# Prologue of a transformer-layer kernel: row normalisation behind its own moments, x loaded first, rotation table in two parts

## What is computed

```python
def _layernorm(x, axis=-1, eps=1e-05):
    return (x - mean(x)) / sqrt(var(x) + eps)
...
q, k, v = proj(Wq, bq), proj(Wk, bk), proj(Wv, bv)
q, k = _apply_rope(q, sin, cos), _apply_rope(k, sin, cos)      # rotation by position
scores = where(pos < 205 or pos >= 1536, q @ k.T * scale, -inf)
attn_out = softmax(scores) @ v @ Wo.T + bo
...
logits = x @ router_w.T
expert, weight = argmax(logits), softmax(top2(logits))[0]
out_e = (silu(x @ gate_w.T) * (x @ up_w.T)) @ down_w.T          # of that expert
...
x = x + attn(xn) + weight * out_e(xn)
```

## Time and profile before

| | us |
|---|---|
| median of 3 runs | 395.14 |
| lowest, highest | 394.01, 395.59 |
| profiled execution | 396.47 |
| its span, first to last instruction | 394.7 |

### The profile page before, as it was taken

How to read it: one execution, slowest core, us unless ns; L and a number is a source line. 1 busy time by engine, 2 the same in 40 slices (tenths; PEclk the granted TensorE clock), 3 DMA queues, 4 the chain that set the end, 5 groups by cost and what they waited for, 6 DMA issues and landing times.

```text
span 394.7 us, 12245 instructions
## 1 busy us (share of the span) xinstructions
PE 370.9 (94%) x4646; PEld 194.1 (49%) x4646; DVE 322.2 (82%) x549; ACT 270.2 (68%) x537; POOL 65.6 (17%) x82
## 2 busy tenths in 40 slices
PE   0999999999999999999999999999999999997896
PEld 0765566766655443444444444445454444432265
DVE  5769789997759888988888888888888898874566
ACT  2534666564448878778787787878888888886910
POOL 5003734431000213032130321300000000000000
PEclk9999999999999999999999999999999999998999
DMA  7998556755111213032130321302102022095626
GB/s 238 407 384 215 145 169 200 215 171 157 41 58 54 70 32 95 11 94 63 41 88 14 99 55 46 92 11 71 55 21 70 25 52 56 17 204 105 101 54 213
DMA packets 30920, 42.53 MB, mean 108 GB/s; under 512 B 10724, under 2 KB 25700, under 8 KB 30048
## 3 DMA queue, kind: packets, MB, share of 16 engines
q1 hardware_dynamic: 29000, 36.71, 32.5%
q0 software_dynamic: 1872, 5.11, 5.1%
HBM read 27.75 MB, written 13.67 MB: 105 GB/s over the span
## 4 chain that ended last, share of the span: by engine, by line
PE 83%; DMA 5%; DVE 4%; issue 3%; ACT 2%; SPq 2%; DVEq 0%; ACTq 0%
PE ps L735 19%; PE ps L713 18%; PE ps L653 17%; PE ps L601 7%; PE ps L528 5%; PE ps L614 5%; PE ps L772 4%; DVE mx L1025 3%; DMA softmax_sums<-o_st 2%; DMA bqk<-bqk_in 2%; PE ps L639 2%; PE ps L517 1%; PE ps L587 1%; PE ps L626 1%; PE ps L510 1%
## 5 line engine op out<-in xcount | busy, mean ns | idle before, releaser
L1025 DVE TENSOR_REDUCE mx<-ps 128x1 f32<-128x717 f32 x232 | 198.6, 899 | 30.6 <-PE ps L653 30.1
L735 PE MATMUL ps<-q_op,k_op 98*32 98x512 bf16 (+1 forms) x1472 | 129.7, 383 | 3.6 <-DMA q_op<-neg_row 1.6
L1307 ACT ACTIVATE probs<-ps 128x512 f32<-128x512 f32 x192 | 103.1, 598 | 19.9 <-PE ps L735 18.1
L653 PE MATMUL ps<-k_op,q_op 96*32 96x512 bf16 (+1 forms) x1856 | 111.2, 315 | 0.4 <-DVE mx L1025 0.3
L653 PEld LDWEIGHTS ps<-k_op,q_op 96*32 96x32 bf16 x1856 | 50.7, 96 | 56.3 <-issue 25.3
L735 PEld LDWEIGHTS ps<-q_op,k_op 98*32 98x32 bf16 (+1 forms) x1472 | 42.3, 96 | 67.0 <-ACT probs L1307 15.0
L713 PE MATMUL ps<-probs,v_op 128*32 128x512 f32 x384 | 50.6, 595 | 0.2 <-ACT o_st L1298 0.2
L1307 ACT ACTIVATE dn<-ps 77x512 f32<-77x512 f32 x64 | 34.8, 595 | 11.6 <-PE ps L735 11.6
L457 POOL COPY v_op<-v_all 128x192 f32<-128x192 f32 x16 | 7.0, 446 | 202.7 <-PE ps L713 202.7
L1307 ACT ACTIVATE gu<-ps 128x512 f32<-128x512 f32 x64 | 34.5, 599 | 9.1 <-PE ps L735 9.1
L1307 ACT ACTIVATE wqk<-ps 128x512 f32<-128x512 f32 x64 | 33.5, 599 | 8.1 <-PE ps L735 8.1
(11 more groups left out here) (127 smaller groups left out, 366.0 us busy)
## 6 DMA issues: line engine op xcount, KB each, us to landing
q_parts<-parts SPq DMA_DIRECT2D x12, 256.0 KB
sorted_results<-ys SPq DMA_DIRECT2D x23, 128.0 KB
q_op<-q_parts SPq DMA_DIRECT2D x15, 192.0 KB
gu<-gu_in SPq DMA_DIRECT2D x1, 2816.0 KB, 13.7
tab<-tab_in SPq DMA_DIRECT2D x1, 2048.0 KB, 11.6
sorted_rows<-xn SPq DMA_DIRECT2D x4, 512.0 KB, 6.1
out<-x_sb SPq DMA_DIRECT2D x8, 256.0 KB, 2.4
q_op<-q_parts SPq DMA_DIRECT2D x15, 128.0 KB
```

The lines of the kernel that those rows point to most:

```text
L653: ins = pe.matmul(ps[r:r + CW, at + c0:at + c0 + n], q_op[slot][0:KR, P * t + r:P * t + r + CW], k_op[slot][0:KR, c0:c0 + n], start=True, ...
L735: ins = pe.matmul(bank(4 + u % RING)[r:r + w, :], k_op[k][:, c0 + r:c0 + r + w], q_op[k][:, QB * b:QB * b + QB], start=True, stop=True)
L1025: dve.tensor_reduce(mx[:, slot, t:t + 1], ps[:, at:at + NK], AX.X, ALU.max).then_inc(max_reduced, 1)
L1307: act.activation(prob[c][0:rows, QB * b:QB * b + QB], bank(4 + u % RING)[0:rows, :], ACT.Exp, scale=SCALE).then_inc(exp_done, 1)
```

## The change

It does six things, all in the prologue and at its edge to the expert stage.

1. DVE's `moments` is split in `moments` (statistics) and `variance`; group 0 is normalised right behind its own variance, and the others one half step later. `ON_DVE = (1, 1, 2, 2)` tiles of the groups are normalised by DVE, the others by ACT (3, 3, 2, 2; before 2, 2, 2, 0), and ACT counts each tile by itself.
2. All of x is issued ahead of the other loads, but for the identity (128 columns of `const`), which goes third. The rest of `const` follows behind the key weights.
3. `wqk` is loaded as keys (ahead) and queries (last of the row); the value weights no longer share a semaphore with the biases.
4. `tab` is loaded as the columns that the keys need (205 and 512, 717 KB together) and, behind the wait for `xs_in[1]` on SP, the 1331 columns between (1331 KB). DVE waits for these ahead of `times_cos(2)`.
5. PE does the logits of rows 0 to 511 behind pair 1, `project(0)` behind pair 2, and one chunk of values behind each of pairs 3 and 4.
6. POOL fills `v_all` with ones first, then the rows of the key operands.

```diff
@@ loads, SP
+                if g == 0:
+                    sp.dma_start(const[:, C_ID:C_ID + P], const_d[:, C_ID:C_ID + P]).then_inc(ident_in, 16)
...
+            tab_v = tab_d.rearrange("p (a n) -> p a n", a=2)
+            for c0, c1 in ((0, START), (S - RECENT, S)):
+                sp.dma_start(tab[:, :, c0:c1], tab_v[:, :, c0:c1]).then_inc(key_tab_in, 16)
...
             sp.wait_ge(xs_in[1], 16)
+            sp.dma_start(tab[:, :, START:S - RECENT], tab_v[:, :, START:S - RECENT]).then_inc(tab_in, 16)
             sp.dma_start(wo[:], wo_d).then_inc(wo_in, 16)
@@ POOL
+            pool.memset(v_all[:], 1.0).then_inc(ones_ready, 1)
+            pool.wait_ge(ones_ready, 1)
             for n in range(RING):
                 pool.memset(k_op[n][KR:KM, :], 1.0).then_inc(ones_ready, 1)
...
-            pool.memset(v_all[:], 1.0).then_inc(ones_ready, 1)
@@ turn_pair, PE
+                g = pair // 2
+                if pair % 2 == 0:
+                    pe.wait_ge(xn_ready, g + 1)
+                pe.wait_ge(xn_on_act, ON_ACT[g] + 2 - ON_DVE[g] if pair % 2 == 0 else ON_ACT[g + 1])
@@ DVE
-            for g in range(1, 4):
-                moments(g)
-                normalize(g - 1)
+            variance(0)
+            normalize(0)
+            moments(1)
+            variance(1)
+            moments(2)
+            normalize(1)
+            variance(2)
+            moments(3)
+            normalize(2)
+            variance(3)
             normalize(3)
...
             turn(1)
+            dve.wait_ge(tab_in, 16)
             times_cos(2)
@@ ACT
             root(0)
-            for g in range(1, 4):
-                root(g)
-                normalize(g - 1)
-                copy_xT(2 * g - 2)
-                copy_xT(2 * g - 1)
+            normalize(0)
+            copy_xT(0)
+            root(1)
+            copy_xT(1)
+            normalize(1)
+            root(2)
+            copy_xT(2)
+            copy_xT(3)
+            normalize(2)
+            root(3)
+            copy_xT(4)
+            normalize(3)
+            copy_xT(5)
             copy_xT(6)
```

More of the change, by code:

```diff
@@ L65 @@
 EARLY_MAX = 6 * 512
+ON_DVE = (1, 1, 2, 2)
+ON_ACT = [sum(4 - n for n in ON_DVE[:g]) for g in range(5)]
 EARLY_TILES = [(0, t) for t in range(NT)] + [(1, t) for t in range(NT // 2)]
@@ L531, in project @@
                     ins.then_inc(proj_ready, 1)
-            pe.wait_ge(const_in, 16)
-            for pair in range(NT // 2):
-                turn_pair(pair)
[L536 to L543, removed]
-                        logits_part(0, m)
-            pe.wait_ge(wv_in, 32)
-            project_v(V_ORDER[0])
+            pe.wait_ge(ident_in, 16)
+            turn_pair(0)
+            turn_pair(1)
+            pe.wait_ge(rt_in, 16)
+            pe.wait_ge(xnT_ready, 2)
+            for m in range(HC):
+                logits_part(0, m)
+            turn_pair(2)
+            pe.wait_ge(wk_in, 32)
+            project(0)
+            turn_pair(3)
+            pe.wait_ge(wv_in, 16)
+            project_v(V_ORDER[0])
+            turn_pair(4)
+            project_v(V_ORDER[1])
+            for pair in range(5, NT // 2):
+                turn_pair(pair)
             for b in range(1, NQB):
@@ L807, in moments, with variance @@
                     step(dve.bn_stats(stats[:, t, :], x_sb[:, t, :]))
+            def variance(g):
                 settle()
@@ L820, in normalize @@
                                          rstd[:, 4 * g:4 * g + 4], ALU.mult, ALU.mult).then_inc(scale_ready, 1)
[L822 removed]
+                for t in range(4 * g, 4 * g + ON_DVE[g]):
                     ins = dve.tensor_scalar(xn[:, t, :], x_sb[:, t, :], mv[:, t, 0:1], rstd[:, t:t + 1],
@@ L1190, in normalize @@
                 act.wait_ge(scale_ready, g + 1)
-                for t in range(4 * g + 2, 4 * g + 4):
-                    ins = act.activation(xn[:, t, :], x_sb[:, t, :], ACT.Identity, bias=shift[:, t:t + 1],
-                                         scale=rstd[:, t:t + 1])
-                ins.then_inc(xn_on_act, 1)
+                for t in range(4 * g + ON_DVE[g], 4 * g + 4):
+                    act.activation(xn[:, t, :], x_sb[:, t, :], ACT.Identity, bias=shift[:, t:t + 1],
+                                   scale=rstd[:, t:t + 1]).then_inc(xn_on_act, 1)
             def biased(u, odd):
```

37 lines of the change are left out of this document (15 added, 22 removed).

## The result

The changed kernel takes 398.33 us (median of 6, 397.68 to 400.27) against 394.69 us (6, 393.13 to 395.59) for the kernel before in the same rounds: a ratio of 1.0102, 95% interval 1.0070 to 1.0134. That is 3.6 us more, where +0.7 was forecast, and beyond the range's end of 397.7. On another chip it was 398.75 to 395.10, a ratio of 1.0096 [1.0067, 1.0125].

A forecast was written before the change was run, and what follows sets the result against it. TensorE was taken as the bound, unbroken from 12.19 us. The larger of -0.35 (prologue) and +0.7 (late table) was added to 395.14, giving 395.8 us; range 393.7 to 397.7.

The forecast's parts named there:

- the table's landing: Edge to expert stage: the table's middle lands at 45.4 us, between 44.8 and 46.8, and VectorE waits for it.
- the issue: SyncE issues the table's middle when the second gather has landed: 39.5 us, between 39.2 and 40.6.
- the duration: Transfer of the table's middle, 1331 KB: 5.9 us, between 5.6 and 6.2.
- rival 3: Table's middle takes 7.5 us amid gathers and key stores, landing at 48.1 if issued at 40.6: 398.5 us; chance 0.14.
- The slack: VectorE's idle time at the expert stage: `times_cos(2)` may start 3.05 us later, at 44.7, with nothing late.
- Whatever is beyond goes through in full: Expert stage: any table delay past 44.7 us reaches TensorE in full, since TensorE gives nothing back from 66 us.
- the larger of two: The end moves by the larger of the prologue's -0.35 us and the table's +0.7 us.
- The head: Prologue: transposes of the logits at 24.05 instead of 24.40 us, 0.35 gained, between -0.9 and +1.1.
- GpSimd's part: Start of prologue: VectorE's variance waits for GpSimd's filling of `v_all`; filled first, variance ends at 5.7 to 5.9, not 6.57.
- 1 (table in time): Expert-stage edge: a 5.1 us transfer or quicker gather leaves the prologue's gain standing, 394.0 to 394.8 us; chance 0.25.
- 2 (the whole early start): Prologue: early clock rise and early `rt` keep TensorE 2.8 us ahead, table in time: 392.3 us; chance 0.08.
- 4: Prologue: ScalarE's order and a late clock lose 0.9 us, gather late, table at 46.6: 397.0 us; chance 0.08.

The follow-up runs named there:

- t1: Changed kernel with the table's middle loaded in two transfers, the 307 columns read first ahead of the other 1024: ratio 1.0013 to the kernel before.
- b0: Kernel before, unchanged, run and profiled a second time: 394.12 us, ratio 0.9983.
- a1: Changed kernel with the table's middle issued at the end of the first row of loads, not behind the second gather: ratio 1.0053 to the kernel before.
- p1: a1 with 24 more, long fulfilled waits on SyncE ahead of the row stores: ratio 1.0017 to the kernel before.
- g1: f1 with router weights behind x's second group, expert down weights behind the second gather, and 24 more fulfilled SyncE waits: ratio 1.0064 to the kernel before.
- u1: f1 with router weights behind x's second group and only 307 middle table columns early, 1024 behind the second gather: 393.59 us, ratio 0.9954.
- f1: a1 with ScalarE normalising ahead of copies, pairs 4 to 7 turned in a row, value chunks placed where TensorE waited: ratio 1.0036 to the kernel before.

## Why the prediction was wrong, point by point

**The step that failed is the table's landing.** Forecast 45.4 with an upper bound of 46.8, measured 48.02, so TensorE lost 2.76 us to it and not 0.7. Two terms: the issue, forecast 39.5, was 40.33, because the second gather was issued at 37.01 instead of 36.3 (head) and took 3.30 instead of some 3.2; and the duration, forecast 5.9 [5.6, 6.2], was 7.69. The duration is the larger miss. I had built it from `wo`'s 3.0 us, for a fifth of the bytes, and the increments of loads in the first row, where no gather runs. The row nearest in kind was the whole table's, 11.6 us amid other traffic, whose share is 7.5; I used it for rival 3 alone and let the range end short of it. That rival (issued 40.6, 7.5 us, landing 48.1, 398.5 us) is what happened. The Trainium skill ("DMA: Bandwidth & Descriptors", Anatomy of one DMA), whose fit is for transfers that GpSimd issues while SyncE issues this one, gave an estimate of 5.1 us, further off still than my 5.9 from the measured 7.69.

**The slack** of 3.05 us was nearly right. Nothing is late up to a `times_cos(2)` at 45.28, which is 3.6 us behind 41.67 and 0.6 more than I took; t1, at 45.60, has a lag no larger than its prologue's. "Whatever is beyond goes through in full" and "the larger of two" held: in four profiles the lag is the start less 45.28, whatever the prologue did. The earlier trace rows carried this part.

**The head** was forecast at -0.35 and came out at +0.39 (-0.64 against b0), inside its bounds, and as the table set the end, it did not count. The forecast gain was itself 0.17 us too large: it set 24.05 against 24.40, which the chain gives, while TensorE's timeline has these transposes from 24.23. Right were: the variance at 5.55 to 5.72 (5.7 to 5.9), the first transpose at 7.15 (7.1), the first copy at 8.27 (8.2), the full clock behind the first logits, `project(0)` at 0.2 each, and both uncovered copies (0.88, 0.69). Wrong was x of group 1: it was there at 7.83, not 7.0, and `rt` followed at 10.99 instead of 10.2. SyncE issued this piece of x 0.5 us later than before (2.25 against 1.74), since the identity is issued ahead of it. The rest is within the scatter: over the thirteen profiles with the identity ahead it landed at 7.03 to 7.88, over the four without at 6.82 to 7.79. The 0.8 us shrank to 0.46 at the transposes of the logits (24.51 to 24.05). GpSimd's part was as read: filled first, `v_all` no longer holds up VectorE's variance, 0.17 us instead of 1.08.

**Not foreseen** was the 0.76 us for the queries' operands, and that the expert weights would be issued later (20.74 against 19.72) behind the row stores. The prediction followed SyncE's queue past the moved transfers only, not past the stores, whose wait moved with ScalarE's order.

**The other rivals.** 1 (table in time) failed on the landing. 2 (the whole early start) failed on the four waits as it said: 3.71 us idle against 3.4 won and spent. 4 asked for a late clock; the full rate came behind the first logits, as forecast. Sum by the measured terms: 394.69 + 2.76 + 0.76 = 398.2; measured 398.33. The table alone would have given 397.45, inside the range: that the time fell beyond its end took the 0.76 us as well, and those were luck.

## What to carry to other kernels

Price a transfer that is moved by a row of the same size amid the same neighbours, not by small ones on empty engines, and load first the slice that the first reader touches: with 307 of the 1331 columns ahead of the others, TensorE lost nothing more to the table. When bytes leave an early row of loads, look at what the issuing queue does with the gap; if its next entries wait for computed rows, the gap stays empty and the late traffic is as dense as before. An earlier start of an engine is only worth what the busy-plus-idle balance up to the next stage shows.

## What the runs showed of the hardware

- One more issue ahead of it put a 256 KB load's own issue back by 0.5 us on SyncE (1.74 to 2.25). Its landing scattered by 0.85 and 0.97 us over the profiles with it and without it (7.03 to 7.88, and 6.82 to 7.79), so the cost of the 64 KB themselves is below what single profiles tell.
- The same four-instruction logits took 1.90 us at TensorE's full rate and 3.56 at its half rate, while the granted clock read 1.00 in both. The rate rose behind about 14.6 us in the changed kernel (first product at 7.15), and in the kernel before (first at 9.94 and 10.01) at 16.8 in one profile and at about 15.0 in the other, with 32.80 and 32.03 us busy up to slot 1. Over all versions this busy time for the same work lay between 31.5 and 33.6 us; I read the spread as the clock's.
- Two issues on SyncE lay 0.44 us further apart or not, depending on 24 fulfilled waits placed far ahead of them (a1 and p1); TensorE waited 0.76 us for their data or not at all, and the head stage began 0.81 us apart.
- The second gather of 128 rows landed 2.7 to 7.2 us after its issue (g1 35.98 to 38.69, u1 36.13 to 38.88, b0 35.86 to 42.20, f1 35.69 to 42.90). It was slowest where the gate and up weights landed last (35.8 us in f1, 34.7 in b0, 30.2 in u1).
